# Sorted experts: router tiles between the first shared blocks, turned rows kept, shared blocks computed by feature

## What is computed

```python
sg = jnp.einsum('td,sdh->tsh', xf, sw1)          # one shared expert, hidden 512
su = jnp.einsum('td,sdh->tsh', xf, sw3)
shared_out = jnp.einsum('tsh,shd->td', jax.nn.silu(sg) * su, sw2)
logits = xf @ router_w.T + experts_bias          # 8 experts
rw, sel = jax.lax.top_k(logits, 2)
rw = jax.nn.softmax(rw)
cw = (jax.nn.one_hot(sel, E) * rw[..., None]).sum(axis=1)
eo = jax.nn.silu(xf @ w1[e]) * (xf @ w3[e])      # each routed expert, hidden 512
return cw-weighted sum of (eo @ w2[e]) + shared_out
```

## Time and profile before

| what | value |
|---|---|
| median of three runs | 3406.27 us |
| the runs | 3396.41, 3406.27, 3411.48 us |
| span of the profiled execution | 3403.5 us (no other time is given for it) |
| PE busy | 3201.0 us, 94% of the span |
| DVE, ACT, POOL busy | 2263.3, 1458.3, 1048.3 us |
| mean granted TensorE clock | 0.967 |
| l2f, first PE instruction to last down | 2293.0 to 2642.7 us |
| l3f, first PE instruction to last down | 3192.6 to 3399.3 us |

### The profile page before, as it was taken

How to read it: one execution, slowest core, us unless ns; L and a number is a source line. 1 busy time by engine, 2 the same in 40 slices (tenths; PEclk the granted TensorE clock), 3 DMA queues, 4 the chain that set the end, 5 groups by cost and what they waited for, 6 DMA issues and landing times. The chain is left out here.

```text
span 3403.5 us, 105614 instructions
## 1 busy us (share of the span) xinstructions
PE 3201.0 (94%) x39150; PEld 2569.5 (75%) x39150; DVE 2263.3 (66%) x7473; ACT 1458.3 (43%) x4212; POOL 1048.3 (31%) x1684
## 2 busy tenths in 40 slices
PE   8979899999996999999999999889999999998899
PEld 6758787788774888888878888776666778877676
DVE  4767326777757988888747777774334577777755
ACT  2325335666632333333336666552111455555432
POOL 0114112333343544444523333343110111114441
PEclk9989899999998999999999999988999999998799
DMA  6643332122103000000011111006111111110333
GB/s 226 219 169 156 115 112 63 56 71 59 64 32 128 3 2 2 2 2 2 2 31 42 52 45 56 2 27 231 47 46 67 36 40 41 43 42 2 99 104 113
DMA packets 145872, 225.26 MB, mean 66 GB/s; under 512 B 14216, under 2 KB 121480, under 8 KB 143816
## 3 DMA queue, kind: packets, MB, share of 16 engines
q1 hardware_dynamic: 138816, 203.16, 18.8%
q0 software_dynamic: 6816, 18.69, 1.5%
HBM read 201.03 MB, written 38.74 MB: 70 GB/s over the span
## 5 line engine op out<-in xcount | busy, mean ns | idle before, releaser
L3385 POOL TENSOR_TENSOR l1fu_second_weighed<-l1fu_second,l1fu_parts 128x256 bf16<-128x256 bf16 x384 | 273.1, 738 | 342.9 <-DVE l1fu_second L3628 336.0
L3437 PEld LDWEIGHTS l1fu_ps_u<-l1f_xnT_all,l1f_key_in 128*128 128x128 f32 x2048 | 249.4, 193 | 17.8 <-issue 11.6
L3437 PE MATMUL l1fu_ps_u<-l1f_xnT_all,l1f_key_in 128*128 (+1 forms) x2048 | 252.1, 277 | 9.1 <-issue 7.5
L3448 PE MATMUL l1fu_ps_y<-l1f_key_out,l1fu_units 128*128 128x256 f32 x1024 | 250.6, 389 | 1.6 <-DVE l1fu_units L3636 1.6
L3448 PEld LDWEIGHTS l1fu_ps_y<-l1f_key_out,l1fu_units 128*128 128x128 f32 x1024 | 185.7, 190 | 33.2 <-issue 6.2
L3501 ACT COPY l1fu_plane<-l1fu_ps_p 128x512 f32<-128x512 f32 x128 | 74.9, 585 | 252.9 <-PE l1fu_ps_p L3427 252.9
L3623 DVE TENSOR_TENSOR l1fu_first<-l1fu_index,l1fu_counted 128x1024 bf16<-128x1024 bf16 x128 | 165.4, 1292 | 20.1 <-PE l1fu_ps_p L3427 18.0
L3509 ACT ACTIVATE l1fu_units<-l1fu_ps_u 128x512 f32<-128x512 f32 x128 | 76.4, 597 | 147.9 <-PE l1fu_ps_y L3448 138.7
L1069 ACT ACTIVATE l1x_scores<-l1x_scores,l1x_minus_big 128x257 f32<-128x257 f32 x256 | 129.1, 516 | 12.0 <-DVE l1x_minus_big L1155 10.4
L1069 ACT ACTIVATE l2x_scores<-l2x_scores,l2x_minus_big 128x257 f32<-128x257 f32 x256 | 129.1, 516 | 12.1 <-DVE l2x_minus_big L1155 10.4
L1069 ACT ACTIVATE l3x_scores<-l3x_scores,l3x_minus_big 128x257 f32<-128x257 f32 x256 | 128.6, 505 | 10.9 <-DVE l3x_minus_big L1155 9.7
(11 more groups left out here) (755 smaller groups left out, 8514.7 us busy)
## 6 DMA issues: line engine op xcount, KB each, us to landing
rows_by_expert<-in_zeros_dram SPq DMA_DIRECT2D x1, 17544.0 KB
l0x_ctxT<-in_ctx_T_dram SPq DMA_DIRECT2D x32, 514.0 KB, 5.3
l0x_ctx_rows<-in_ctx_dram SPq DMA_DIRECT2D x64, 256.0 KB, 3.5
l0f_w<-in_L_ffn_w_dram SPq DMA_DIRECT2D x16, 1024.0 KB, 5.1
l1x_ctx_sb<-in_ctx_T_dram SPq DMA_DIRECT2D x60, 256.0 KB, 3.3
l2x_ctx_sb<-in_ctx_T_dram SPq DMA_DIRECT2D x60, 256.0 KB, 3.4
l3x_ctx_sb<-in_ctx_T_dram SPq DMA_DIRECT2D x60, 256.0 KB, 2.8
l1x_mask_raw<-in_mask_int_dram SPq DMA_DIRECT2D x16, 514.0 KB, 4.2
```

What stands on the lines that cost most here:

```text
L3385: last = nc.gpsimd.tensor_tensor(second_weighed[:, k % 2, part], second[:, k % 2], parts[:, 1 - par, part, TC * k:TC * k + TC].unsqueeze(2 ...
L3437: last = nc.tensor.matmul(ps_u[:, k % 2, j, :], key_in[:, c, JS * k + j, :], xnT_all[:, c, bass.ts(tile, P)], start=(c == 0), stop=(c == C ...
L3448: last = nc.tensor.matmul(ps_y, units[:, k, j, :], key_out[:, JS * k + j, :], start=(k + j == 0), stop=(k == K - 1 and j == JS - 1))
```

## The change

It does five things. (1) The router is spread out: four tiles (`LED`) go through PE ahead of block 0, and the other twelve between the matrices of blocks 0 to 2, one after gate, one after up, two at the end of the turn (`PIECES`, `late_tiles`). The same pieces are put into ACT's list. (2) The turned rows of all 16 tiles are kept, in three places (`xnT`), so shared blocks need no `turn_rows`. (3) Shared blocks are computed by feature (`up_shared`): 128x128 pieces of the matrix stand as weights, and the turned rows, 128 columns, stream. The result has features on the partitions, so no `turn_hidden` is needed, and ACT writes it into `hiddenT` directly (`hidden_of`). (4) `down` of a shared block comes one turn after its `up`, that of a routed block two turns after, as before (`downs`). (5) DVE's and PE's steps of the router are put into later turns: ranks(n-1) and positions(n-1) in turns 1 to 4, best_two(n) in turns 0 to 3, normed_tiles(2) and (3) in turns 0 and 1, the block tables in turns 4 and 5, the shares in turn 7. The waits are changed to match.

```diff
+    LED = 4
+    PIECES = (1, 1, 2)
...
-        ps_logits = [ps_l, ps_d]
+        ps_logits = [ps_l, ps_h]
...
+        def hidden_of(n):
+            w = weights_of(n)
+            if is_routed(n):
+                return hidden[:, n % 2, 0:w.hidden]
+            return hiddenT[:, n % 2, 0:w.hidden // P].rearrange("p h n -> p (h n)")
+
+        def downs(n):
+            return [m for m in range(max(n - 2, 0), min(n, N)) if m + (2 if is_routed(m) else 1) == n]
+
+        def late_tiles(n, piece):
+            first = LED + n * sum(PIECES) + sum(PIECES[:piece])
+            return range(min(first, NT), min(first + PIECES[piece], NT))
...
+            def router_tiles(tiles_now):
+                for i in tiles_now:
+                    turn_xn(i)
+                    if i:
+                        router_logits(i - 1)
+                    if i == NT - 1:
+                        router_logits(i)
...
+            def up_shared(n, a):
+                w, i = ws, order[n][1]
+                if a == 0:
+                    if n == 0:
+                        pe.wait_ge(ws.loaded, ws.all_loaded)
+                    pe.wait_ge(s["xnT_ready"], i + 1)
+                    if n and not is_routed(n - 1):
+                        pe.wait_ge(s["activated"], swiglu_blocks(n))
+                    else:
+                        after(pe, s["hidden_ready"], n)
+                else:
+                    after(pe, s["hidden_ready"], n)
+                dst = (ps_g, ps_u)[a]
+                for hc in range(w.hidden // P):
+                    for c in range(C):
+                        last = nc.tensor.matmul(dst[:, hc * P:hc * P + P], w.up[:, 0, a, c, hc * P:hc * P + P],
+                                                xnT(i)[:, c, :], start=(c == 0), stop=(c == C - 1))
+                last.then_inc(s["gate_up_ready" if a == 0 else "up_ready"], 1)
...
-                pe.wait_ge(s["hiddenT_ready"], n + 1)
+                if is_routed(n):
+                    pe.wait_ge(s["hiddenT_ready"], order[n][1] + 1)
+                else:
+                    pe.wait_ge(s["hidden_ready"], n + 1)
                 after(pe, s["y_ready"], n)
...
             for n in range(N):
                 at[n] = expert_of_block(n)
-                up(n, at[n])
-                if n:
+                if is_routed(n):
+                    up_routed(n, at[n])
+                else:
+                    up_shared(n, 0)
+                    router_tiles(late_tiles(n, 0))
+                    up_shared(n, 1)
+                    router_tiles(late_tiles(n, 1))
+                if n and is_routed(n - 1):
                     turn_hidden(n - 1)
-                if n + 1 < N:
-                    turn_rows(n + 1)
-                if n > 1:
-                    down(n - 2, at[n - 2])
-                if n < 2:
-                    ranks(n + 2)
+                if n + 1 < N and is_routed(n + 1):
+                    turn_rows(order[n + 1][1])
+                if 1 <= n <= NG:
+                    ranks(n - 1)
+                for m in downs(n):
+                    down(m, at[m])
+                router_tiles(late_tiles(n, 2))
...
             def activate(n):
                 w = weights_of(n)
                 act.wait_ge(s["gate_up_ready"], n + 1)
 
-                after(act, s["hidden_turned"], n - 1)
-                rows = hidden[:, n % 2, 0:w.hidden]
+                after(act, s["down_ready"], n - 1)
+                if is_routed(n):
+                    after(act, s["hidden_turned"], order[n][1] - 1)
+                rows = hidden_of(n)
...
-            normed_tiles(2)
-            best_two(0)
-            normed_tiles(3)
-            positions(0)
-            best_two(1)
-            positions(1)
-            best_two(2)
             for n in range(N):
                 gate_hidden(n)
                 if is_routed(n):
                     name_home(order[n][1])
-                if n:
+                if n and is_routed(n - 1):
                     keep_hiddenT(n - 1)
-                if n > 1:
-                    keep_y(n - 2, merged_by(n))
+                for m in downs(n):
+                    keep_y(m, merged_by(n))
                 if is_routed(n):
                     dump_empty(order[n][1])
                 if n < 2:
-                    positions(n + 2)
-                if n == 0:
-                    best_two(3)
-                if n == 2:
+                    normed_tiles(n + 2)
+                if 1 <= n <= NG:
+                    positions(n - 1)
+                if n < NG:
+                    best_two(n)
+                if n == NG:
                     block_table()
                     block_rows()
```

More of the change, by code:

```diff
@@ L2812, in ranks, with turn_rows @@
                 last.then_inc(s["ranked"], 1)
[L2814 to L2819, removed]
-                else:
-                    rows = xn_all[:, i, :]
-                pe.wait_ge(s["xsT_ready"], max(n - 1, 0)) if n > 1 else pe.wait_ge(s["xnT_ready"], NT)
+            def turn_rows(b):
+                pe.wait_ge(rows_loaded[b % RING], 16 * (b // RING + 1))
+                if b < 2:
+                    pe.wait_ge(s["xnT_ready"], NT)
+                else:
+                    pe.wait_ge(s["xsT_ready"], b - 1)
                 for c in range(C):
-                    last = nc.tensor.transpose(ps_x[:, n % 2, c * P:c * P + P], rows[:, c * P:c * P + P], ident)
+                    last = nc.tensor.transpose(ps_x[:, b % 2, c * P:c * P + P], xs[:, b % RING, c * P:c * P + P], ident)
                 last.then_inc(s["turned"], 1)
@@ L2846, in up @@
                     for c in range(C):
-                        last = nc.tensor.matmul(dst[:, 0:w.hidden], xsT[:, n % 2, c, :],
+                        last = nc.tensor.matmul(dst[:, 0:w.hidden], xsT[:, b % 2, c, :],
                                                 w.up[:, at, a, c, :].rearrange("p e n -> p (e n)"),
@@ L2852, in turn_hidden @@
             def turn_hidden(n):
+                b = order[n][1]
                 pe.wait_ge(s["hidden_ready"], n + 1)
-                after(pe, s["hiddenT_ready"], n)
-                for hc in range(weights_of(n).hidden // P):
+                if b == 0:
+                    pe.wait_ge(s["logits_kept"], NT)
+                after(pe, s["hiddenT_ready"], b)
+                for hc in range(wr.hidden // P):
                     last = nc.tensor.transpose(ps_h[:, hc * P:hc * P + P], hidden[:, n % 2, hc * P:hc * P + P], ident)
@@ L2871, in _ @@
             pe.wait_ge(s["weights_loaded"], 32)
[L2872 to L2881, removed]
+            router_tiles(range(LED))
             at = {}
@@ L2914, in keep_logits, with keep_rowsT @@
                         then["exp_ready"], 1)
[L2916 to L2920, removed]
+            def keep_rowsT(b):
+                act.wait_ge(s["turned"], b + 1)
+                if b > 1:
+                    act.wait_ge(s["gate_up_ready"], FIRST + b - 1)
+                    after(act, s["up_ready"], swiglu_blocks(FIRST + b - 1))
+                nc.scalar.copy(xsT[:, b % 2].rearrange("p c n -> p (c n)"), ps_x[:, b % 2, 0:D]).then_inc(
                     s["xsT_ready"], 1)
@@ L3104, in gate_hidden @@
                     dve.wait_ge(s["up_ready"], swiglu_blocks(n + 1))
-                    nc.vector.tensor_tensor(hidden[:, n % 2, 0:w.hidden], hidden[:, n % 2, 0:w.hidden],
-                                            ps_u[:, 0:w.hidden], ALU.mult).then_inc(s["hidden_ready"], 1)
+                    rows = hidden_of(n)
+                    nc.vector.tensor_tensor(rows, rows, ps_u[:, 0:w.hidden], ALU.mult).then_inc(s["hidden_ready"], 1)
             def keep_hiddenT(n):
                 w = weights_of(n)
-                dve.wait_ge(s["hidden_turned"], n + 1)
+                dve.wait_ge(s["hidden_turned"], order[n][1] + 1)
                 after(dve, s["down_ready"], n - 1)
```

60 lines of the change are left out of this document (32 added, 28 removed).

## The result

The changed kernel takes 3533.09 us (median of 4 runs, 3526.61 to 3541.88) against 3401.34 for the kernel before on the same chip: ratio 1.0392, 95% interval 1.0371 to 1.0414, so **3.9% slower**. The forecast was 3519 us (+3.3%), with a range of 3480 to 3560. It was a sum of +113 us; the ratio makes it 0.0392 x 3401.3 = 133 us, and the two profiled executions stand 3529.0 - 3403.5 = 125.5 us apart.

A forecast was written before the change was run, and what follows sets the result against it. PE's own instruction stream was taken to bound the routed stretch, so any wait there is paid in full. Routed blocks +104, leading part +16 and trailing part -7 gave +113 us on 3406.3: 3519 us, range 3480 to 3560.

The forecast's parts named there:

- Routed blocks, l2f: In l2f's routed blocks the activation waits for down of block n-2, idling PE 1.68 us in 37 blocks: +62 us.
- Routed blocks, l3f: The same added wait in l3f's routed blocks, 1.14 us in each of 37 blocks: +42 us.
- Leading part: Blocks ahead of the routed ones, router moved: scatter 8.4 us later in l2f, PE waits for rows; +16 us, both layers.
- The clock term: Leading part: after 16 us of idling PE does about 4 us of matmuls at half speed, +2 us per layer.
- Trailing part: Nine shared blocks behind the routed ones save 0.51 us each, less 0.9: 3.7 per layer, -7 us for both.
- one wait for block 46: The first trailing block waits once more for down(44), in front of block 47: 0.9 us per layer.
- B: Rival: the clock falls to 1.2 GHz in the routed stretch, 80 us more in l3f (3599), 215 in l2f; chance 0.10.
- C: Rival: the wait in activate costs nothing, leaving 3415 us, or 3394 with the leading part low; chance 0.06.
- D: Rival: shared blocks' weights are reloaded for each 128 columns without overlap, 82 us more, 3601; chance 0.02.

The follow-up runs named there:

- e8: e6 with the last two routed downs between gate and up of the first two trailing blocks, and their keep_y ahead of gate_hidden; ratio 0.9941 to the kernel before.
- e2: The kernel before with one wait added: in routed blocks ACT waits for down_ready >= n-1 ahead of the activation; ratio 1.0362 to the kernel before.
- e1: The changed kernel with the wait for down_ready kept for shared blocks alone, routed blocks waiting for hidden_turned only; ratio 1.0028 to the kernel before.
- e5: e1 with positions(n-1) ahead of keep_y and normed_tiles in DVE's turn; ratio 1.0025 to the kernel before.
- e6: e1 with five router tiles ahead, ranks, best_two and positions earlier, eight shared blocks each side, four tiles combined per turn; ratio 0.9966 to the kernel before.

## Why the prediction was right, and where it was off

The sign, the mechanism of the largest term and its place were right. The sum was 113 us where the stages of the profile show 125.7. By the prediction's own steps:

- **Routed blocks, l2f: 62 forecast, 70.4 measured** (37 turns in 285.69 us, before 215.26). This is the largest miss of size. A turn grew by 1.91, not 1.68. The idle time runs over the links of the forecast: down's tail 0.16, silu 0.60 and gating 0.69 as taken; PE to ACT 0.09, not 0.03; ACT to DVE 0.03, not 0.06; DVE to PE 0.24, not 0.14. That is 1.81, and the gate after an idle stretch takes 1.98 where it took 1.88, 0.10 more. The sum had no term for this last part. DVE to PE had been 0.14 in the earlier trace rows with the same form of gating; why it is 0.24 here is open.
- **Routed blocks, l3f: 42 forecast, 42.3 measured** (122.42 against 80.13). A turn grew by 1.14 on average, as forecast. This is in part luck: PE to ACT was 0.09 instead of 0.03, the gate took 0.10 longer, and the copy started 0.10 before activate's record ended, where the sum had it 0.06 behind: +0.06 and +0.10 against -0.16.
- **Leading part: +16 forecast, +13.3 measured.** In l2f the first routed gate comes 72.9 us after the first router tile, before 65.5: +7.4, where the forecast was 7.4 and 2 for the clock (its last step, 2363.8 + 0.2 + 1.73, gives 2365.7 and not 2365.9, so 7.2). The way there is the forecast's: the scatter starts at 2316.9 (forecast 2317.1), issued as one train; PE is done with its shared work at 2349.2 (2347) and idles 13.2 us (16). Timeline of PE in after:

```profile
2334.71 0.41 PE L2840 MATMUL l2f_ps_r<-l2f_chosen_in,const 128*128 128x32 f32 x2 [1.54 <-DVE l2f_earlier_in L3053]
...
2335.40 3.61 PE L2921 MATMUL l2f_ps_d<-l2fs_w_down,l2f_hiddenT 128*128 128x256 f32 x8
...
2362.31 0.69 PE L2857 MATMUL l2f_ps_x<-const,l2f_xs 128*128 128x128 f32 x2 [13.15 <-DMA l2f_xs<-rows_by_expert]
2362.79 3.62 PE L2921 MATMUL l2f_ps_d<-l2fs_w_down,l2f_hiddenT 128*128 128x256 f32 x8
2366.20 1.93 PE L2897 MATMUL l2f_ps_g<-l2fr_w_up,l2f_xsT 128*128 x4
```

  The rows are asked for at 2360.25 and used at 2362.31, so 0.75 sooner than the forecast's 2361.0, and in 2.1 us instead of the 2.8 that I took. The clock term came nearly as forecast, since the down after the idle stretch takes 3.62, 1.7 more than at full clock; the sooner and quicker rows paid for most of it. Up to the gate of block 9, where the routed turns begin to wait, l2f lost 6.0 (forecast 5.6 + 2) and l3f 7.3 (6.2 + 2).
- **Trailing part: -7 forecast, -0.2 measured** (from the first trailing gate to the start of the last down 57.2 us against 57.1 in l2f, 54.8 against 55.1 in l3f). The saving per block is there, 5.30 a turn, 0.52 less than a turn of 5.82. What was missed is the seam. In turn 47 PE does two downs, of block 45 (routed, two turns late) and block 46 (shared, one turn late). All engines in after:

```profile
2672.58 1.89 PE L2921 MATMUL l2f_ps_d<-l2fr_w_down,l2f_hiddenT 128*128 x8
2674.57 0.60 ACT L2983 ACTIVATE l2f_hiddenT<-l2f_ps_g 128x512 f32<-128x512 f32 x1 [5.78 <-PE l2f_ps_d L2921]
2675.20 0.69 DVE L3163 TENSOR_TENSOR l2f_hiddenT<-l2f_hiddenT,l2f_ps_u 128x512 f32<-128x512 f32 x1 [4.76 <-ACT l2f_hiddenT L2983]
2675.81 0.42 DVE L3181 COPY l2f_y<-l2f_ps_d 128x256 f32<-128x256 f32 x1
...
2676.37 3.23 PE L2921 MATMUL l2f_ps_d<-l2fs_w_down,l2f_hiddenT 128*128 128x256 f32 x8 [1.90 <-DVE l2f_y L3181]
```

  The second down needs the first one's bank emptied (keep_y, on DVE); keep_y stands behind the gating of block 47, that behind its activation, and that waits for the first down. So PE idles 1.90 and comes back at the low clock: the down takes 3.23 instead of 1.89 and the gate behind it 2.39 instead of 1.95. The forecast counted one wait for block 46 (0.9 per layer) and looked no further into the next turn. In l3f the stall of 1.89 is there too, without the low clock (down 1.97), but the wait for block 46 was mis-sized as well, 2.12 for 0.9. ACT in after:

```profile
3474.38 1.28 ACT L2983 ACT_TABLE_LOAD   x1 [5.12 <-PE l3f_ps_d L2921]
3475.67 0.60 ACT L2983 ACTIVATE l3f_hiddenT<-l3f_ps_g 128x512 f32<-128x512 f32 x1
```

  Ahead of the first silu behind the gelus of the routed blocks ACT has a record ACT_TABLE_LOAD of 1.28 us. Behind the added wait it falls into the time in which PE stands still; the sum had no term for it. e8, where the order of the seam is mended on PE and DVE, shows it without the stalls.

Together +8.2 and +0.3 in the routed blocks, -2.7 in the leading part and +6.8 in the trailing one are, to the rounding, the 12.7 us between 113 and 125.7. That the total is only 13 us off is helped a little by the leading part, which was off the other way.

**The rivals.** B fell: the granted clock of both routed stretches is 1.00, with PE idle for 1.65 of every 7.7 us and 0.87 of every 3.3. The Trainium skill's page TensorE: Matmul & The Clock Gate describes under A second HAM failure mode: psum-queue depth-cycling a kernel whose short idles between groups of matmuls made the clock swing; this trace does not show that for the routed blocks. C fell with the turns of 7.73 and 3.30 us, and e2 answers it alone: the wait costs its full price. D fell with the 5.30 us of a shared turn: sixteen records with changing weights take 1.79 (3329.21 to 3331.00 in e8), 0.112 a record. The Trainium skill's 107 ns for a load of 128 columns (same page, LDWEIGHTS) is a little less than the 112 ns at which the records stand here, and the row was the better base for the sum.

The step of the prediction that failed is the trailing part, where the forecast of a gain ended in none; the largest term, the wait in the routed blocks, was found with its place and its way, and came out 12% too small in l2f (62 for 70.4).

## What to carry to other kernels

When a wait is widened so that a new kind of block is safe, write it for that kind alone; in a loop where one engine is busy all the time, a wait for its last work of the turn lays the whole chain of handoffs bare in every turn (here 1.9 us in 37 turns and 1.1 in 37). Work taken off the bound engine ahead of a long transfer only pays if the start of that transfer moves forward too: look for what stands in front of the first issue on the engine that releases it. And where two kinds of blocks meet whose steps lag by different numbers of turns, write out the turn in which both fall due: here that seam took back nearly all that the shorter trailing blocks had saved.

## What the runs showed of the hardware that was not expected

The clock after a short stall is not the same each time. In l2f the fourth group of ranks waits 1.54 us in after and in e1; the down behind it takes 3.61 us in after, 2.63 in e1. In e5, with 0.32 us of waiting, it takes 1.97. In l3f the wait in the same place is 2.39 us in after and in e1, and down takes 1.97 in after, 3.76 in e1; and 2.47 us in e6 and in e8, with a down of 3.76 and one of 1.97. The window over the slow one in after, 3 us long:

```profile
2335.50:2338.50 3.00, 3.00 (x9) 2.38 (x9) 0.00 (x0) 0.00 (x0) 2.25 (x3) 0.51 1.01 390
```

A mean of 0.51 is the low level, 1.2 GHz, for nearly all of it. And in the routed stretches of after, where a stall of 1.65 or 0.87 us comes in every turn, no fall is seen. What decides between these cases no run here tells. In e6 the 2.47 us of waiting cost another 2.7 us at the low clock (3.76 for 1.97 and 2.83 for 1.95), and in e8 nothing; so a forecast of stalls should give the clock's share as a range from nothing to about that much beside each.
